# ScalarE issues the loads of the next rows of x and the next context in the middle of a sequence's score loop

## The reference

```python
# x (16, 512, 256), ctx_512 (16, 64, 128)
h = _layernorm(x)
q, k, v = heads(h @ Wq + bq), heads(h @ Wk + bk), heads(h @ Wv + bv)        # 16 heads of 16
y = softmax(causal(q k^T / 4)) v
qc, kc, vc = heads(h @ Wcq + bcq), heads(ctx @ Wck + bck), heads(ctx @ Wcv + bcv)
y = y + softmax(qc kc^T / 4) vc                                           # cross attention
x = x + tanh(g_xattn[0]) * (y @ Wp + bp)
# then, on layernorm(x): top-2 of 16 experts (the last one is the identity), each silu(gate) * up, down,
# plus a shared expert whose gate is a causal convolution of width 3
x = x + tanh(g_ffn[0]) * ffn(_layernorm(x))
```

## Time and profile before

| what | value |
|---|---|
| median of 3 runs | 1580.44 us (1579.65 to 1582.32) |
| the profiled execution | 1578.51 us |
| its span in the trace | 1576.8 us |
| PE, DVE, ACT, POOL busy | 94%, 76%, 55%, 56% of the span |
| mean granted TensorE clock | 0.983 |
| chain that ended last, by engine | PE 73%, DVE 12%, ACT 6%, DMA 3% |
| attention phase | from the begin to about 1200 us |

### The profile page before, as it was taken

The page is one execution under the profiler, slowest core; times in us unless marked ns, Lnnn a source line. Parts: engine busy times, 40 slices in busy tenths (PEclk is TensorE's granted clock), DMA queues, the critical chain, the costliest instruction groups (busy, mean ns, idle before and its releaser), DMA issues.

```text
span 1576.8 us, 35849 instructions
## 1 busy us (share of the span) xinstructions
PE 1481.2 (94%) x11219; PEld 950.3 (60%) x11219; DVE 1192.8 (76%) x3093; ACT 867.3 (55%) x1823; POOL 890.6 (56%) x1529
## 2 busy tenths in 40 slices
PE   4899999999999999999999999999988999999696
PEld 2455555555555555555555565555554988998474
DVE  5777787878787787878787877878844666776897
ACT  3365666656665666666656656666550444443555
POOL 2244465564646565565646465565645565776673
PEclk8999999999999999999999999999999999999899
DMA  6844555545455555446455555455564676555797
GB/s 168 198 133 126 146 160 155 153 134 179 143 163 147 155 157 152 139 150 176 139 153 164 148 154 163 129 155 167 177 197 144 200 251 210 172 176 166 255 309 247
DMA packets 190613, 268.30 MB, mean 170 GB/s; under 512 B 33048, under 2 KB 136224, under 8 KB 190432
## 3 DMA queue, kind: packets, MB, share of 16 engines
q1 hardware_dynamic: 154208, 196.35, 43.7%
q0 software_dynamic: 12960, 36.51, 6.4%
q10 hardware_dynamic: 23264, 33.19, 6.3%
HBM read 160.28 MB, written 105.66 MB: 169 GB/s over the span
## 4 chain that ended last, share of the span: by engine, by line
PE 73%; DVE 12%; ACT 6%; DMA 3%; issue 3%; POOL 2%; SPq 0%; DVEq 0%; POOLq 0%; ACTq 0%
PE scalar_bank L1355 10%; PE pv_self L1429 9%; PE scalar_bank L1366 8%; PE vector_bank L1909 7%; PE vector_bank L1403 6%; PE vector_bank L1345 4%; PE vector_bank L1314 4%; PE vector_bank L1472 4%; DVE nmax L1199 4%; PE vector_bank L1400 4%; PE pv_cross L1412 3%; PE vector_bank L1445 2%; PE scalar_bank L1896 2%; ACT q L808 2%; ACT parts L817 2%
## 5 line engine op out<-in xcount | busy, mean ns | idle before, releaser
L1199 DVE TENSOR_REDUCE nmax<-vector_bank 128x1 f32<-128x384 f32 (+4 forms) x832 | 512.3, 641 | 92.4 <-PE vector_bank L1403 91.0
L869 ACT ACTIVATE pt<-scalar_bank 128x512 f32<-128x512 f32 x640 | 355.1, 600 | 220.4 <-PE scalar_bank L1366 216.7
L700 POOL TENSOR_SCALAR_AFFINE_SELECT pt<-pt 128x256 f32<-128x256 f32 (+1 forms) x640 | 228.7, 373 | 215.7 <-ACT pt L869 208.5
L1366 PE MATMUL scalar_bank<-stack 99*64 99x512 bf16 (+4 forms) x1280 | 282.3, 320 | 4.5 <-DMA stack<-max_scratch 2.7
L1403 PE MATMUL vector_bank<-stack 96*128 96x128 bf16 (+3 forms) x1024 | 244.7, 303 | 0.0
L1400 PE MATMUL vector_bank<-tri,ident_b 128*128 128x128 bf16 (+2 forms) x704 | 175.5, 249 | 14.8 <-DMA stack<-qk_scratch 10.9
L1355 PE MATMUL scalar_bank<-xnT,w_qk 128*128 128x512 f32 x384 | 185.2, 607 | 1.1 <-ACT xnT L794 1.1
L1743 POOL DMA_INDIRECT rows<-pt x142 | 138.8, 977 | 80.1 <-issue 62.4
L659 POOL DMA_INDIRECT rows<-xn,slot x128 | 134.0, 1047 | 51.8 <-issue 27.4
L1429 PE MATMUL pv_self<-pt,vst 128*32 128x512 f32 (+3 forms) x2048 | 161.0, 438 | 0.1
L1400 PEld LDWEIGHTS vector_bank<-tri,ident_b 128*128 128x128 bf16 x704 | 67.6, 97 | 151.4 <-DVE nmax L1199 81.5
(11 more groups left out here) (304 smaller groups left out, 2647.1 us busy)
## 6 DMA issues: line engine op xcount, KB each, us to landing
qk_scratch<-parts SPq DMA_DIRECT2D x31, 1200.0 KB, 4.6
stack<-qk_scratch SPq DMA_DIRECT2D x120, 192.0 KB, 3.0
pt<-rows SPq DMA_DIRECT2D x142, 132.0 KB, 2.5
stack<-qk_scratch SPq DMA_DIRECT2D x248, 72.0 KB, 2.6
pt<-rows SPq DMA_DIRECT2D x16, 1024.0 KB, 6.2
stack<-qk_scratch SPq DMA_DIRECT2D x124, 128.0 KB, 3.0
stack<-qk_scratch SPq DMA_DIRECT2D x240, 36.0 KB, 2.2
xt<-in_x_dram ACTq DMA_DIRECT2D x15, 512.0 KB, 5.4
```

The lines of the kernel that those rows point to most:

```text
L700: pool.affine_select(out=v, in_=v, compare_op=ALU.is_ge, fill=0.0, base=0, pattern=pat, channel_multiplier=-1).then_inc(masked, 1)
L869: act.activation(dst, bank(kind, ("st", c, k))[:, :], ACT.Exp, scale=SCALE).then_inc(scalar_drained, 1)
L1199: dve.tensor_reduce(dst, src, axis=AX, op=ALU.max, negate=True).then_inc(vector_drained, 1)
L1366: return pe.matmul(out, stack[c][0:rows, head, key0:key0 + nk], stack[c][0:rows, head, q0:q0 + nq], start=True, stop=True, **kw)
```

## The change

The call of `next_rows` moves: from behind `transposed`, at a body's begin, to behind the exponential of slot 8 of the first half. The two waits inside `next_rows` are dropped, since what they waited for lies before that exponential's own scores.

```diff
             def next_rows(kind, b):
 
-                act.wait_ge(xn_ready, LN.upto(kind, b, 0))
                 act.dma_start(xt[:, :, :], x[min(b + 2, B - 1)].rearrange("(t p) c -> p t c", p=P)).then_inc(x_in, 16)
                 if b + 2 < B:
-                    act.wait_ge(scalar_filled, SU.upto(kind, b, ("xT", QT - 1)))
                     for i in range(2):
                         act.dma_start(ctile[i * TC:(i + 1) * TC, :], ctx[b + 2]).then_inc(ctx_in, 16)
...
                 for c in range(KC):
                     if nxt and c == 0:
                         transposed(kind, b)
-                        if cur:
-                            next_rows(kind, b)
...
                         exponentials(kind, b, c, k)
                         if nxt and k < 2:
                             middle_part(kind, b, c, 2 + k)
+                        if nxt and (c, k) == (0, 8):
+                            next_rows(kind, b)
                         if prev:
                             finished_rows(kind, b, c, k)
```

## The result

The changed kernel takes **1600.62 us** (median of 5 runs, 1598.76 to 1603.49), the kernel before 1580.44 us in the same comparison (5 runs, 1578.22 to 1582.32). The ratio is 1.0131 with a 95% interval of 1.0116 to 1.0146: 20.2 us slower, where the forecast was 10.0 us slower, to 1590.4.

A forecast was written before the change was run, and what follows sets the result against it. TensorE was taken to bound the kernel, with 73% of the chain. Thirteen bodies at 0.69 us (9.0 us) plus 1.0 us in the first body, on the median of 1580.44, gave 1590.4 us; range 1580.0 to 1602.0.

The forecast's parts named there:

- The gain at the begin: Body's begin: the issues leaving there lay under TensorE's projection, so removing them gains 0.
- `xt` stays covered: Load of x lands at about 719.0, its first reader is at 725.87: 6.9 us of cover, cost 0.
- `stack` stays covered: Reads of `stack` behind the write of the projections: a write up to 3.7 us late costs TensorE 0.
- the first rival: Slot 8: DMAs without a wait pass the waiting exponential, so no change, 1580.4 us; chance 0.12.
- the term of 0.69 us in a body: Bodies 1 to 13: issues behind slot 8 delay exponentials, so TensorE's slot 13 starts 0.69 us late; 9.0 us in all.
- the slowest pair seen, 1.91 us: Context loads' two issues: if each pair took this long, the loss would be 1.38 us in a body, 17.9 us.
- a collision of the load of x with the maxima's rows: First body: the 512 KB of x under way with those rows, between 0 and perhaps 3 us, taken as 1.0.
- the rival that I had given 0.06: 14 bodies: write of the projections lands late, TensorE waits for `stack`; at worst 1.7 us each, 1614 us; chance 0.06.
- the faster case: Bodies: clock dips stay away and slot 12's stall doesn't come, giving 1577.1 us; chance 0.04.

## Why the prediction was right, and where it was wrong

**Right: the mechanism, its place and its direction.** The gain at the begin is nil: in body 11 L808 still follows its idle time of 2.13 us, though the queue ahead of it is now empty.

```profile
858.66 0.69 ACT L808 ACTIVATE q<-scalar_bank,bias 128x512 f32<-128x512 f32 x1 [2.13 <-PE scalar_bank L1353]
```

The loads start with the exponential of slot 8; slot 9 is held until the last issue has ended; the next one who waits is TensorE at slots 12 and 13; body 14, with one issue, loses nothing (71.00 us before and after). `xt` stays covered: the statistics L963, now first read at 886.65 in body 11, wait for no load of x but the kernel's very first, as before. `stack` stays covered in bodies 1 to 13: behind the shift of 0.93 us no row of TensorE in body 11 comes later still. (The 11.0 us that the page of after gives to row maxima waiting for `stack`, 10.9 before, are a single wait ahead of the first body, and say nothing of this.) The first body is another matter, below.

**Right: the first rival fails.** The DMAs carry no wait and might have run ahead of the exponential. They did not: 873.46, with slot 8's start, not 872.37. The same holds in bodies 1 to 14 of every kernel run here with loads behind slot 5, 7 or 8. Where the exponentials stand back to back, at slot 13 and in the first body, the loads start up to 0.35 us ahead of the exponential they stand behind, but not before the one ahead of it. "Perfetto Trace Analysis" of the Trainium skill (section on the DVE / Act engine instruction) would have had them start early, since waits are held in a queue of their own; the traces speak against it for DMAs on this queue behind an exponential that waits.

**Wrong: the size of the term of 0.69 us in a body,** 9.0 us over bodies 1 to 13, and with it the forecast of 10.0 us for the whole. It measured 14.3 to 16.5 us, 1.10 to 1.27 in a body; the whole was 20.2. (1600.62 lies within the stated range up to 1602.0, which was drawn for slow issues in every body and 3 us in the first one; the range's width, and not the sum, held it.) The three parts:

- The pair's issues in a quiet body take 1.30 us here instead of 1.22: 0.08 us. Both neighbours of the pair have a part in it: with the write ahead but not the load of x it takes 1.14 us, with the load of x ahead but not the write 1.18.
- The forecast dated slot 13's scores before the change wrongly. It took half of the chain's 0.55 us for two slots and got 715.745; the timeline has these scores at 715.64. So slot 13 had 0.10 us less to spare, and this is the larger part of what a quiet body lost over the forecast. The evenly spread exponentials (0.52 us apart, where back to back they stand 0.49 apart) worked the other way by 0.03. TensorE's row of slot 13 before, then slot 10's exponential and slot 13 in body 11 after:

```profile
715.64 0.38 PE L1366 MATMUL scalar_bank<-stack 99*64 99x512 bf16 x2
```

```profile
875.71 0.59 ACT L867 ACTIVATE pt<-scalar_bank 128x512 f32<-128x512 f32 x1
```

```profile
876.35 0.41 PE L1364 MATMUL scalar_bank<-stack 99*64 99x512 bf16 x2
```

Slot 13 thus starts 2.89 us behind slot 8 instead of 2.04, 0.85 us late, and 0.05 us after the exponential it waits for, close to the 0.04 that I had used. The 0.14 us ahead of slot 12 have no part in this, since slot 13 has its own wait. Another 0.07 us come later: 0.02 at the cross products and 0.05 at the row maxima 5 us on (720.89 before, 881.66 after); no row shows why.

- That gives the 0.94 us of body 11 (0.91 to 0.94 in the quiet bodies; with 0.93, 12.1 us in all). The rest are slow pairs: over the quiet body's 1.29 us the thirteen pairs have 4.4 us too much in the first profile of the changed kernel, and 2.2 and 2.9 us in the two others (means 1.63, 1.46 and 1.51 us). The forecast held the slowest pair seen, 1.91 us, as a bound for all and took the median for the sum. Four pairs of the first profile passed that bound (1.98 to 2.54 us). But the median belonged to a place where the DMA engines had no write of 1200 KB ahead of it. What I did not ask was what else these issues wait for; I asked that only of the transfers. The kernel with the write held back shows the write as the main cause: without it 1.18 us in nearly every body. It is not the only one: one pair took 1.69 us there, and behind slot 13, 5.5 us after the write, single pairs still took 1.66 to 2.22 us. What slows those stays open, and so does the way in which the write does it.

**The remainder goes with the clock.** The bodies' 18.0 us of the two profiles are 16.5 of the change and 1.5 of dips (three in the profile after, one of them in body 1, against two). Another 4.5 us lie where the change does nothing: 1.9 ahead of the first body, where the granted clock up to 59 us was 0.86 against 0.88, and 2.6 behind body 14, where it was 0.95 against 0.97. That the clock made all of these 4.5 us is an inference from these rows. The two later comparisons give 1.0109 and 1.0113, 17.7 and 18.4 us on the 1627 us of their chips, against 20.2 in the first; the intervals overlap. Of these 18 to 20 us, 14.3 to 16.5 are accounted for body by body.

**Wrong: the cause in the first body.** I gave it 1.0 us for a collision of the load of x with the maxima's rows. Those rows came no later: slot 12's scores start 16.3 to 18.0 us into the body in the three profiles of the changed kernel, 17.2 and 18.2 before. What came late is the write of the projections, the rival that I had given 0.06 and had looked for in all bodies. SyncE's first read of `stack` waits for that write. It starts 7.45 us after the write's issue in the third profile of the changed kernel and 5.38 in the second of the kernel before (SyncE's timelines, changed first):

```profile
76.12 0.39 SPq L443 DMA_DIRECT2D qk_scratch<-parts  x1
83.57 1.28 SPq L456 DMA_DIRECT2D stack<-qk_scratch  x3
```

```profile
74.33 0.39 SPq L443 DMA_DIRECT2D qk_scratch<-parts  x1
79.71 1.28 SPq L456 DMA_DIRECT2D stack<-qk_scratch  x3
```

The first user of these rows, the row maxima between the projections of c = 1, then has TensorE standing for 2.95 us instead of 0.66 (changed first; the bracket names no releaser, since the record of the product that waits is missing):

```profile
92.82 0.39 PE L1401 MATMUL vector_bank<-stack 96*128 96x128 bf16 x4 [2.95 <-issue]
```

```profile
89.26 0.33 PE L1403 MATMUL vector_bank<-stack 96*128 96x128 bf16 x3 [0.66 <-issue]
```

Both of these first bodies run at a granted clock of 1.00 throughout, and they take 66.87 and 65.29 us: 1.6 us. In the other profiles TensorE is at its lower clock for a part of this body (0.74 from 75 to 85 us in the first profile of the changed kernel), and the lengths, 67.95 and 68.21 against 67.16, don't separate the two. TensorE's wait does: 1.97, 2.60 and 2.95 us in the three profiles of the changed kernel, 2.92 with x alone at slot 8, 0.77 and 0.82 with the block behind slots 13 and 5, 1.13 with the context's pair alone at slot 8, and in the kernel before none and 0.66. So the 1.0 us was near in size by luck: its mechanism was another. That would also be a part of what x alone lost.

In bodies 1 to 13 the late write did not come, and the faster case came nowhere.

## What to carry to other kernels

An issue of a DMA is work of the queue it stands in, and the exponential behind it waited here for its end (0.05 us from one to the other). Put it where the engine idles anyway, and read the price as what the next instructions come late less what their users can bear: here the same three loads cost nothing behind slot 5 or 13, and 0.9 us in a body and more behind slot 8. An issue's duration is not a constant of its shape: take it from rows where the DMA engines are as busy as they will be in the new place. And read the start of an instruction from its own row: halving a merged piece of a chain cost 0.10 us in a body here.

## What the hardware showed that was not expected

- The pair of issues of 32 KB each, right behind the issue of x: 1.18 us with no write ahead, mostly 1.3 to 1.5 us when a 1200 KB write was issued 2.6 us before the block, about 2.0 us (1.98 to 2.08, one 1.79) when 1.5 to 2.4 us before, 2.04 to 2.54 us when 0.4 to 1.1 us before, and once 3.43 us. Single pairs took 1.66 to 2.22 us 5.5 us behind the write too. The issue of 512 KB ahead of the pair stays at 0.37 to 0.40 us in all of these.
- A handoff from ScalarE to a waiting TensorE took 0.14 us at slot 12 and 0.05 us at slot 13, in the same bodies, in the changed kernel and with a computation in place of the issues alike. With the block at slot 7, the wait at slot 11 shows 0.05 us. What makes slot 12 differ is not shown.
- The clock dips of about 1.7 us hit other bodies in each profile, but nearly always the same place within a body (31.7 to 34.1 us into it).

The chain of waits of that kernel, at slot 11:

```profile
943.66 0.05 issue
943.71 0.39 PE scalar_bank L1364 x2
```
